# Moving one weight check and the first part of a tile across the block boundary

## The chip, the cores and the metric

The kernel runs on one core of one Trainium2 chip. The metric is the device time of the whole launch in microseconds (us); lower is better. A matmul engine (TensorE, PE in the rows), a vector engine (VectorE, DVE), a scalar engine (ScalarE, ACT), a general engine (GpSimd, POOL) and SyncE (SP, which here only issues DMAs) run their own instruction streams in order and meet through semaphores.

## The reference

The reference is a residual feed-forward layer whose input is a gated bidirectional recurrence along the sequence, for 4 batches of 1024 positions and 1024 channels:

```python
x = x + _L0_ffn_ref(_L0_cond_ref(x, fside, fside, w, u, cond), W1, W2)
# _L0_cond_ref: k = v = fside, r = x
ek = exp(min(k, 30)); ekv = ek * v
a, b = a * decay + ekv_t, b * decay + ek_t     # forward and backward over the 1024 positions
num = nf + nb - ekv + euk * v;  den = df + db - ek + euk
out = sigmoid(r) * (num / max(den, 1e-8)) * (0.8 + 0.2 * tf)
# _L0_ffn_ref: W1 (4096 x 1024), W2 (1024 x 4096), entries t * 2^-e, t in {-1, 0, 1}, e in 0..4
h = einsum('bsd,fd->bsf', x, W1)
a = gelu(clip(round(h / 0.1), ...) * 0.1)
return einsum('bsf,df->bsd', a, W2)
```

## The kernel before

**Blocks and tiles.** The 4 batches are cut into two halves of 512 positions each, which gives 8 blocks (n = 0 to 7). A block has 8 channel tiles of 128 channels x 512 positions. While block n goes through the feed-forward part, the recurrence of block n+1 is computed tile by tile on VectorE and ScalarE, so that TensorE finds its operands ready at the next block. Tiles are numbered through, g = 8 * block + t. In the even blocks a tile is "late" and needs the sums over the first half of the sequence as well, which costs two more activations on ScalarE (`exps`) and two more VectorE instructions (`weigh`).

**What a tile needs.** On ScalarE `tile_group(g)` issues the exponentials of tile g (`exps`), the logarithm and exponential that invert the denominator of tile g-1 (`reciprocal`, left out where g is the first tile of its block) and the exponential of the gate (`gate_exp`). On VectorE a tile is four parts: `part(0, g)` weighs the values, `part(1, g)` is the forward scan, `part(2, g)` the backward scan, `part(3, g)` the sums that free the tile's buffers. `mix(t, p, ...)` inside a block calls `part(p, g0 + t)`, where g0 = 8 * (n + 1) is the first tile of the next block; it does nothing in the last block.

**Feed-forward.** Each matmul is done in fp16 pieces (high and low), and most of the products are arranged as Winograd-like products of seven, with sums of operands made on VectorE. In a block from n = 1 on, TensorE starts with `products_15(n, 0)` (32 matmuls of 256 columns, line 754), whose first product is copied by ScalarE from one PSUM bank to another (`seed`, line 1098), and then does `products_26(n, 0)` (32 more), which accumulates on top of that copy and so waits for it: `pe.wait_ge(s_seed, q + 1)`. Then come `products_15(n, 1)`, `products_73(n, 0)`, `products_26(n, 1)`, `product_4(n, 0)` and so on. `product_4` waits for VectorE's `quantise22` (line 1622). At the end of a block the outputs 0 to 7 are made (line 897) and VectorE adds each to the residual and stages it (`residual_sum`, line 1698).

**Operands of the next block.** `operands_hi(n + 1, q)` on ScalarE (lines 1083 to 1086) and `convert(n + 1, q)` on VectorE (lines 1550 to 1565) make the matmul operands of quarter q of the next block, q = 0 to 3.

**The checks.** The kernel is exact only if the weights are multiples of 1/64 that fit in int8. So 64 slices of W1 and W2 (512 KB each) are checked on the way, 8 to a block, numbered `at` = 0 to 63. A check is a load into one buffer, `chk_full` (SyncE, `load_check`, line 502), a cast to int8 on ScalarE (`check_i8`, line 1183) and a comparison on VectorE that overwrites the buffer (`check`, line 1717). There is one buffer for it, so the load of check `at` waits until the comparison of `at - 1` is done:

```python
def load_check(at):
    if at > 0:
        sp.wait_ge(s_chk, at)
```

**Order.** All orders are written out by hand, in one stream for each engine. SyncE issues every load of the kernel in one order: the ring of eight weight slots (`ring_load`), the tiles, the residuals, the checks and the stores. Near the boundary its stream is, at the end of block n: store and residual loads, `load_check(at + 6)`, two ring loads; and at the start of block n+1: a ring load, `load_tile(g0 + 1)`, a ring load, then `load_check(at - 1)` with the new block's numbers. With `at` = 8 * n, the check called `at + 6` at the end of block n is the one called `at - 2` in block n+1.

Of the kernel before, what the change touches and what calls it, by code (L numbers as in the profile page):

```python
# [38 lines left out]
def adaln_ffn_kernel(nc, x, fside, cond, w, u, w1, w2, out):  # L39
    B, HALVES, CT, _, T = x.shape  # L40
# [5 lines left out]
    BLOCKS = B * HALVES  # L46
# [14 lines left out]
    with ExitStack() as ctx:  # L61
# [215 lines left out]
        def hid(n, s):  # L277

            return CHAIN * (n - 1) + (s if s <= SPLIT else s + 2)
# [724 lines left out]
        def _(act_e):  # L1004
# [52 lines left out]
            def tile_group(g):  # L1057

                exps(g, g - 1 if g % CT else g)
                if g % CT:  # L1060
                    reciprocal(g - 1, s_gate, g)
                gate_exp(g)
# [10 lines left out]
            def operands_hi(n, q):  # L1073
                g, at = CT * n + 2 * q, KH * (n - 1) + q
                slot = m_slot(g)
                act_e.wait_ge(s_out, g + 2)
                if n == 1:
                    act_e.wait_ge(s_h0, FT)
                    for k in range(2):
                        act_e.wait_ge(s_wstore[k], 16 * STEPS)  # L1080
                else:
                    act_e.wait_ge(s_p4, CHAIN * (n - 1))
                sc.activation(mo[:, B11, q, 0, :], m_quads[:, slot, 0, :], ACT.Copy).then_inc(s_mohi, 1)
                sc.activation(mo[:, B21:B22 + 1, q, 0, :], m_quads[:, slot, 2:4, :], ACT.Copy).then_inc(s_mohi, 1)
                act_e.wait_ge(s_t, 3 * at + 3)
                sc.activation(mo[:, T1:T4 + 1, q, 0, :], tt, ACT.Copy).then_inc(s_mohi, 1)
# [90 lines left out]
            def check_i8(at):  # L1177
                n = at // DT
                act_e.wait_ge(s_chkload, 16 * (at + 1))
                act_e.wait_ge(s_gelu, half_of(n, SPLIT - 1 if n > 0 and at % DT < 2 else LAST, 1) + 1)  # L1180
                if at > 0:
                    act_e.wait_ge(s_chk, at)
                sc.activation(chk_i8, chk_full[:, :], ACT.Copy, scale=W_SCALE).then_inc(s_chki8, 1)  # L1183
# [27 lines left out]
            def chained_block(n, nxt, g0, at):  # L1211
                seed(hid(n, 0))
                spill_p5(hid(n, 0))
                check_i8(at - 2)
                quantise11(n, 0)
                seed(hid(n, 1))
                spill_p5(hid(n, 1))
                check_i8(at - 1)
                quantise12(n, 0)
                if nxt:  # L1220
                    tile_group(g0 + 1)
                gelu(n, 0, 0)
                quantise11(n, 1)
                quads_hi_11(n, 0)
                for s in range(2, SPLIT + 1):
                    quantise21(n, s - 2)
                    gelu(n, s - 2, 1)
                    seed(hid(n, s))
                    quads_hi_2(n, s - 2)
                    spill_p5(hid(n, s))  # L1230
                    quads_hi_t(n, s - 2)
                    quantise12(n, s - 1)
                    gelu(n, s - 1, 0)
                    quantise11(n, s)
                    quads_hi_11(n, s - 1)

                quantise21(n, SPLIT - 1)
                gelu(n, SPLIT - 1, 1)
                quads_hi_2(n, SPLIT - 1)
                quads_hi_t(n, SPLIT - 1)  # L1240
                seed(part_y(n, 0))
                quantise12(n, SPLIT)
                gelu(n, SPLIT, 0)
                act_hi(n, SPLIT, 0)
                spill_p5(part_y(n, 0))
                if nxt:
                    tile_group_between(g0 + 2)
                quantise21(n, SPLIT)
                gelu(n, SPLIT, 1)
                act_hi(n, SPLIT, 1)  # L1250
                seed(part_y(n, 1))
                check_i8(at)
                spill_p5(part_y(n, 1))
                if nxt:
                    tile_group_between(g0 + 3)
                check_i8(at + 1)
                seed(hid(n, SPLIT + 1))
                spill_p5(hid(n, SPLIT + 1))
                if nxt:
                    tile_group(g0 + 4)  # L1260
                quantise11(n, SPLIT + 1)

                seed(hid(n, SPLIT + 2))
                spill_p5(hid(n, SPLIT + 2))
                if nxt:
                    tile_group(g0 + 5)
                quantise12(n, SPLIT + 1)
                gelu(n, SPLIT + 1, 0)
                quantise11(n, SPLIT + 2)
                act_hi(n, SPLIT + 1, 0)  # L1270
                quantise21(n, SPLIT + 1)
                gelu(n, SPLIT + 1, 1)
                seed(hid(n, LAST))
                act_hi(n, SPLIT + 1, 1)
                spill_p5(hid(n, LAST))
                quantise12(n, SPLIT + 2)
                gelu(n, SPLIT + 2, 0)
                quantise11(n, LAST)
                act_hi(n, SPLIT + 2, 0)

                quantise21(n, SPLIT + 2)
                gelu(n, SPLIT + 2, 1)
                act_hi(n, SPLIT + 2, 1)
                if nxt:
                    tile_group_between(g0 + 6)
                quantise12(n, LAST)
                gelu(n, LAST, 0)
                act_hi(n, LAST, 0)
                quantise21(n, LAST)
                gelu(n, LAST, 1)  # L1290
                act_hi(n, LAST, 1)
                if nxt:
                    operands_hi(n + 1, 0)
                check_i8(at + 2)
                if nxt:
                    tile_group_between(g0 + 7)
                    operands_hi(n + 1, 1)
                check_i8(at + 3)
                check_i8(at + 4)
                if nxt:  # L1300
                    reciprocal(g0 + 7, s_gate, g0 + 8)
                    operands_hi(n + 1, 2)
                    if n + 2 < BLOCKS:
                        tile_group(g0 + CT)
                    operands_hi(n + 1, 3)
                check_i8(at + 5)
                if not nxt:
                    check_i8(at + 6)
                    check_i8(at + 7)

            hidden_block0(CT)
# [11 lines left out]
            reciprocal(CT + 7, s_gate, CT + 8)  # L1323
            check_i8(5)
            operands_hi(1, 3)
            tile_group(2 * CT)
            for n in range(1, BLOCKS):
                chained_block(n, n + 1 < BLOCKS, CT * (n + 1), DT * n)
# [40 lines left out]
        def _(dve):  # L1369
# [149 lines left out]
            def part(p, g):  # L1519

                last = g - 1 if g % CT else None
                if p == 0:
                    weigh(g)
                if p == 1:
                    forward(g, last)
                if p == 2:
                    backward(g, last)
                if p == 3:
                    sums(g)
# [224 lines left out]
            def output_block0(g0):  # L1754
                weight_sums2(0)
                convert(1, 0)
                check(0)
                residual_sum(0, 0)
                part(3, g0 + 4)
                residual_sum(0, 1)  # L1760
                part(0, g0 + 5)
                check(1)
                convert(1, 1)
                weight_sums2(1)
                part(1, g0 + 5)
                residual_sum(0, 2)
                check(2)
                part(2, g0 + 5)
                part(3, g0 + 5)
                weight_sums2(2)  # L1770
                residual_sum(0, 3)
                part(0, g0 + 6)
                check(3)
                part(1, g0 + 6)
                part(2, g0 + 6)
                residual_sum(0, 4)
                part(3, g0 + 6)
                weight_sums2(3)
                part(0, g0 + 7)
                check(4)  # L1780
                part(1, g0 + 7)
                residual_sum(0, 5)
                part(2, g0 + 7)
                part(3, g0 + 7)
                convert(1, 2)
                divide(g0 + 7)
                check(5)
                convert(1, 3)
                residual_sum(0, 6)
                part(0, g0 + CT)  # L1790
                residual_sum(0, 7)

            def chained_block(n, nxt, g0, at):
                def mix(t, *parts):
                    if nxt:
                        for p in parts:
                            part(p, g0 + t)

                seed_u4(hid(n, 0))
                check(at - 2)  # L1800
                mix(0, 1, 2)
                quantise22(n, 0)
                check(at - 1)
# [93 lines left out]
                    convert(n + 1, 3)  # L1897
                    check(at + 5)
                residual_sum(n, 6)
                if n + 2 < BLOCKS:  # L1900
                    part(0, g0 + CT)
                if nxt:
                    residual_sum(n, 7)

            hidden_block0(CT)
# [142 lines left out]
```

## Time and profile before

| | |
|---|---|
| time, median of 3 runs | 1751.11 us (1750.88 to 1751.9) |
| time of the profiled execution | 1751.11 us |
| its span, first to last instruction | 1748.8 us |
| TensorE busy | 1655.3 us (95% of the span) |
| VectorE busy | 1292.6 us (74%) |
| ScalarE busy | 933.8 us (53%) |
| mean granted TensorE clock | 0.986 |
| DMA queue of SyncE | 351.86 MB, 60.6% of 16 engines |

The profiled execution took 1751.11 us, of which 1748.8 us lie between its first and last instruction. A busy share is the share of the span in which at least one instruction of the engine ran. The time in brackets at the end of a row of the timeline is the idle time of that engine just ahead of the row, with the instruction that ended it.

### The profile page before, as it was taken

What the parts mean: (1) busy time and instruction counts of PE and PEld (TensorE: products, weight loads), DVE (VectorE), ACT (ScalarE), POOL (GpSimd) and SP (SyncE); (2) the same over time, 40 slices, a digit from 0 to 9 for tenths busy, and PEclk for the clock granted to TensorE, in tenths of its full rate; (3) what the DMA queues carried; (4) which work ended last, traced back from release to release, by engine and by line L of the source; (5) the groups of instructions that cost most, each with busy time, mean ns of one, the idle gap of its engine ahead of it and who ended that gap; (6) DMA issues with size and microseconds to landing.
All of it is one profiled execution on the core that took longest, in us unless ns stands there. A gap on an engine that the chain in (4) does not pass through costs nothing. (4 is left out here: it accounts for less than half of the span.)

```text
span 1748.8 us, 30785 instructions
## 1 busy us (share of the span) xinstructions
PE 1655.3 (95%) x12258; PEld 1201.0 (69%) x12258; DVE 1292.6 (74%) x1787; ACT 933.8 (53%) x1450; POOL 24.6 (1%) x44
## 2 busy tenths in 40 slices
PE   1579999899999999999999999999999999999998
PEld 0134444688748886688847887488866888478874
DVE  8977877589697867888787876978778776755222
ACT  3457522574746646385655646467464755455141
POOL 0000020000000000000000000000000000000000
PEclk9789999999999999999999999999999999999999
DMA  9858785768556684757747585676847677465744
GB/s 246 196 159 241 282 298 190 247 195 288 175 211 213 217 268 136 262 183 269 241 142 252 183 271 167 217 233 222 286 137 256 185 251 232 158 206 181 234 135 158
DMA packets 153461, 376.97 MB, mean 216 GB/s; under 512 B 15328, under 2 KB 44256, under 8 KB 152800
## 3 DMA queue, kind: packets, MB, share of 16 engines
q1 hardware_dynamic: 150624, 351.86, 60.6%
q0 software_dynamic: 2688, 23.07, 5.8%
q8 instruction: 99, 1.62, 0.4%
q14 instruction: 50, 0.41, 0.1%
HBM read 347.61 MB, written 67.11 MB: 237 GB/s over the span
## 5 line engine op out<-in xcount | busy, mean ns | idle before, releaser
L754 PE MATMUL ps<-mo,w_ring 128*128 128x256 f16 x6272 | 698.7, 273 | 13.1 <-ACT ps L1098 5.7
L754 PEld LDWEIGHTS ps<-mo,w_ring 128*128 128x128 f16 x6272 | 613.6, 98 | 93.7 <-issue 16.0
L897 PE MATMUL ps<-act,w_ring 128*128 128x512 f16 x1760 | 383.3, 380 | 0.0
L817 PE MATMUL ps<-act,w_ring 128*128 128x256 f16 x3136 | 348.1, 273 | 0.0
L817 PEld LDWEIGHTS ps<-act,w_ring 128*128 128x128 f16 x3136 | 306.0, 98 | 36.3
L897 PEld LDWEIGHTS ps<-act,w_ring 128*128 128x128 f16 x1760 | 172.0, 98 | 203.4
L1654 DVE SCALAR_TENSOR_TENSOR act<-a,act 128x1024 f16<-128x1024 f32 x72 | 88.0, 1222 | 95.9 <-ACT act L1158 95.9
L1183 ACT ACTIVATE q<-tt 128x1024 int8<-128x1024 f32 x64 | 67.2, 1050 | 160.7 <-DMA tt<-in_w_dram 160.7
L1148 ACT ACTIVATE a<-q 128x1024 f32<-128x1024 int16 x128 | 135.3, 1057 | 15.7 <-DVE act L1654 10.7
L1098 ACT ACTIVATE ps<-ps 128x512 f32<-128x512 f32 x70 | 40.7, 581 | 153.3 <-PE ps L754 89.5
L1717 DVE SCALAR_TENSOR_TENSOR tt<-q,tt 128x1024 f32<-128x1024 int8 x64 | 78.1, 1221 | 49.0 <-ACT q L1183 49.0
L883 PE MATMUL ps<-act,w_ring 128*128 128x512 f16 x512 | 110.8, 380 | 3.0 <-DVE xy L1698 3.0
L1610 DVE SCALAR_TENSOR_TENSOR ps<-sp,ps 128x512 f32<-128x512 f32 x70 | 48.5, 693 | 85.7 <-issue 43.3
L731 PE MATMUL ps<-mo,w_ring 128*128 128x512 f16 x128 | 42.7, 511 | 71.5 <-DVE mo L1539 71.5
L883 PEld LDWEIGHTS ps<-act,w_ring 128*128 128x128 f16 x512 | 50.0, 98 | 63.7 <-issue 3.4
L1512 DVE SCALAR_TENSOR_TENSOR ND<-EE,bonus,ND 128x1024 f32<-128x1024 f32 x64 | 81.9, 1280 | 1.6
L744 PE MATMUL ps<-mo,w_ring 128*128 128x512 f16 x384 | 83.0, 380 | 0.0
L731 PEld LDWEIGHTS ps<-mo,w_ring 128*128 128x128 f16 x128 | 15.5, 125 | 98.3 <-issue 51.3
L1492 DVE TENSOR_TENSOR_SCAN ND<-decay,back,ND 128x512 f32<-128x512 f32 x64 | 81.9, 1280 | 0.6
L1496 DVE TENSOR_TENSOR_SCAN ND<-decay,back,ND 128x512 f32<-128x512 f32 x64 | 81.7, 1276 | 0.0
L1665 DVE TENSOR_TENSOR tt<-a 128x1024 f32<-128x1024 f32 x28 | 34.3, 1225 | 58.8 <-ACT a L1148 58.8
L1158 ACT ACTIVATE act<-a 128x1024 f16<-128x1024 f32 x72 | 75.8, 1053 | 1.4
(121 smaller groups left out, 1653.4 us busy)
## 6 DMA issues: line engine op xcount, KB each, us to landing
w_ring<-w1s SPq DMA_DIRECT2D x168, 512.0 KB, 4.8
w_ring<-w_half SPq DMA_DIRECT2D x130, 512.0 KB, 5.1
tt<-in_w_dram SPq DMA_DIRECT2D x64, 512.0 KB, 5.3
w_ring<-w2s SPq DMA_DIRECT2D x56, 512.0 KB, 4.9
V<-in_fside_dram SPq DMA_DIRECT2D x64, 256.0 KB, 5.8
R<-in_x_dram SPq DMA_DIRECT2D x64, 256.0 KB, 5.9
w_half<-in_w_dram POOLq DMA_DIRECT2D x16, 1024.0 KB, 8.2
xy<-in_x_dram SPq DMA_DIRECT2D x64, 256.0 KB, 4.9
```

The lines of the kernel that those rows point to most:

```text
L744: mm = pe.matmul(bank[4 * (s % 2) + j][:, :], w1_ring[:, k, f, c, :], mix0[:, c, p, :], start=(c == 0 and p == 0), stop=(c == CT - 1 and p ...
L754: mm = pe.matmul(dst[:, f, :], wp_ring[:, k, r, f, q, :], mo[:, op, q, p, :], start=(fresh and f == 0 and q == 0 and p == 0), stop=(q == K ...
L817: mm = pe.matmul(dst[:, i, :], wy_ring[:, k, i, 2 * s + j, :], ao[:, s, op, j, p, :], start=(fresh and i == 0 and s == 0 and j == 0 and p ...
L883: mm = pe.matmul(y_ps[y][:, :], w2_ring[:, k, f, :], act[:, FPS * s + j, p, :], start=(h == 0 and f == 0 and p == 0), stop=(h == 1 and f = ...
L897: mm = pe.matmul(bank[d][:, :], w2_ring[:, k, FPS * (s - SPLIT) + j, :], act[:, act_at(n, s) + j, p, :], start=(s == SPLIT and j == 0 and ...
L1148: sc.activation(a32[:, 2 * h:2 * h + 2, :], q16[:, s % 2, 2 * h:2 * h + 2, :], ACT.Gelu_apprx_tanh, scale=QSTEP).then_inc(s_gelu, 1)
L1158: sc.activation(act[:, f:f + 2, 0, :], a32[:, 2 * h:2 * h + 2, :], ACT.Copy, scale=ACT_SCALE).then_inc(s_ahi, 1)
L1492: v.tensor_tensor_scan(DEN[:, k, :][:, ::-1], dec(b, c), DEN[:, k, :][:, ::-1], back[:, k, 1:2], ALU.mult, ALU.add).then_inc(s_dbwd, 1)
L1496: v.tensor_tensor_scan(NUM[:, k, :][:, ::-1], dec(b, c), NUM[:, k, :][:, ::-1], back[:, k, 0:1], ALU.mult, ALU.add).then_inc(s_nbwd, 1)
L1512: v.scalar_tensor_tensor(out=ND[:, k, :, :], in0=EE[:, k, :, :], scalar=bonus[:, b, c:c + 1], in1=ND[:, k, :, :], op0=ALU.mult, op1=ALU.ad ...
L1654: v.scalar_tensor_tensor(out=act[:, f:f + 2, 1, :], in0=a32[:, 2 * h:2 * h + 2, :], scalar=ACT_SCALE, in1=act[:, f:f + 2, 0, :], op0=ALU.m ...
L1717: v.scalar_tensor_tensor(out=chk_full[:, :], in0=chk_i8, scalar=1.0 / W_SCALE, in1=chk_full[:, :], op0=ALU.mult, op1=ALU.not_equal, accum_ ...
```

## The change

Three things move, and nothing is added or removed. No load is moved on SyncE.

1. Check 6 of a block (`at + 6`, on ScalarE and on VectorE) is done at the end of its own block and no longer at the start of the next one. On ScalarE it used to stand behind the next block's first `seed` and `spill_p5`; it now stands ahead of them. On VectorE it used to stand behind `seed_u4(hid(n, 0))`; it now stands ahead of `residual_sum(n, 7)` of the block before. This holds for the seven boundaries into blocks 1 to 7.
2. On ScalarE `tile_group(g0 + CT)`, the first tile of the block after the next, moves from between `operands_hi(n + 1, 2)` and `operands_hi(n + 1, 3)` to behind check `at + 6`. In block 0 it stood behind `operands_hi(1, 3)` already, and check 6 now comes ahead of it.
3. On VectorE `part(0, g0 + CT)` moves from ahead of `residual_sum(n, 7)` to the first place of the next block, where it is written `mix(0, 0)`.

```diff
@@ ScalarE, chained_block, start
                 seed(hid(n, 0))
                 spill_p5(hid(n, 0))
-                check_i8(at - 2)
                 quantise11(n, 0)
@@ ScalarE, chained_block, end
                 if nxt:
                     reciprocal(g0 + 7, s_gate, g0 + 8)
                     operands_hi(n + 1, 2)
-                    if n + 2 < BLOCKS:
-                        tile_group(g0 + CT)
                     operands_hi(n + 1, 3)
                 check_i8(at + 5)
+                check_i8(at + 6)
+                if n + 2 < BLOCKS:
+                    tile_group(g0 + CT)
                 if not nxt:
-                    check_i8(at + 6)
                     check_i8(at + 7)
@@ ScalarE, after block 0
             check_i8(5)
             operands_hi(1, 3)
+            check_i8(6)
             tile_group(2 * CT)
@@ VectorE, output_block0
                 residual_sum(0, 6)
-                part(0, g0 + CT)
+                check(6)
                 residual_sum(0, 7)
@@ VectorE, chained_block, start
+                mix(0, 0)
                 seed_u4(hid(n, 0))
-                check(at - 2)
                 mix(0, 1, 2)
@@ VectorE, chained_block, end
                 residual_sum(n, 6)
-                if n + 2 < BLOCKS:
-                    part(0, g0 + CT)
                 if nxt:
+                    check(at + 6)
                     residual_sum(n, 7)
```

## Rows read from the trace of the kernel before

**Rows 1.** Waits of TensorE from 330 us on: total us, times, longest.

```profile
PE ps L754 <- DVE q L1622: 4.4, 6, 0.9
PE ps L754 <- ACT ps L1098: 3.0, 3, 1.4
```

**Rows 2.** Timeline of TensorE, starts of blocks 2 to 7 (start us, us, what).

```profile
522.26 26.36 PE L754 MATMUL ps<-mo,w_ring 128*128 128x256 f16 x240
550.03 3.65 PE L754 MATMUL ps<-mo,w_ring 128*128 128x256 f16 x32 [1.40 <-ACT ps L1098]
...
726.87 26.36 PE L754 MATMUL ps<-mo,w_ring 128*128 128x256 f16 x240
...
930.27 26.62 PE L754 MATMUL ps<-mo,w_ring 128*128 128x256 f16 x240
...
1135.11 29.86 PE L754 MATMUL ps<-mo,w_ring 128*128 128x256 f16 x272
...
1337.71 22.54 PE L754 MATMUL ps<-mo,w_ring 128*128 128x256 f16 x205
...
1540.59 19.60 PE L754 MATMUL ps<-mo,w_ring 128*128 128x256 f16 x178
```

**Rows 3.** Timeline of ScalarE at the boundary into block 2.

```profile
518.71 0.61 ACT L1031 ACTIVATE EE<-V 128x512 f32<-128x512 f32 x1
...
520.55 0.40 ACT L1083 ACTIVATE mo<-m_st 128x256 f16<-128x256 f32 x1
...
524.21 0.58 ACT L1098 ACTIVATE ps<-ps 128x512 f32<-128x512 f32 x1
...
529.67 1.06 ACT L1183 ACTIVATE q<-tt 128x1024 int8<-128x1024 f32 x1 [3.11 <-DMA tt<-in_w_dram]
530.63 0.58 ACT L1119 ACTIVATE q<-ps 128x512 int16<-128x512 f32 x1
```

**Rows 4.** Timeline of SyncE: issue of the loads of checks 6 and 7.

```profile
525.70 0.33 SPq L502 DMA_DIRECT2D tt<-in_w_dram  x1
...
532.02 0.33 SPq L502 DMA_DIRECT2D tt<-in_w_dram  x1
```

**Rows 5.** Timeline of VectorE: checks 5 and 7 at the same boundary.

```profile
524.45 1.22 DVE L1717 SCALAR_TENSOR_TENSOR tt<-q,tt 128x1024 f32<-128x1024 int8 x1
...
539.36 1.22 DVE L1717 SCALAR_TENSOR_TENSOR tt<-q,tt 128x1024 f32<-128x1024 int8 x1 [1.78 <-ACT q L1183]
```

**Rows 6.** Timeline of ScalarE: a late tile's group, and check 6 into blocks 3 to 7.

```profile
720.35 0.61 ACT L1027 ACTIVATE EKP<-VP 128x512 f32<-128x512 f32 x1
...
723.32 0.40 ACT L1083 ACTIVATE mo<-m_st 128x256 f16<-128x256 f32 x1
...
731.75 1.06 ACT L1183 ACTIVATE q<-tt 128x1024 int8<-128x1024 f32 x1 [0.59 <-DMA tt<-in_w_dram]
...
938.04 1.06 ACT L1183 ACTIVATE q<-tt 128x1024 int8<-128x1024 f32 x1 [3.22 <-DMA tt<-in_w_dram]
...
1139.77 1.06 ACT L1183 ACTIVATE q<-tt 128x1024 int8<-128x1024 f32 x1 [0.37 <-DMA tt<-in_w_dram]
...
1344.73 1.06 ACT L1183 ACTIVATE q<-tt 128x1024 int8<-128x1024 f32 x1 [2.73 <-DMA tt<-in_w_dram]
...
1545.24 1.06 ACT L1183 ACTIVATE q<-tt 128x1024 int8<-128x1024 f32 x1 [0.36 <-DMA tt<-in_w_dram]
```

**Rows 7.** Timeline of TensorE: three stretches after an idle wait, one without.

```profile
57.07 5.95 PE L731 MATMUL ps<-mo,w_ring 128*128 128x512 f16 x16 [6.91 <-DVE mo L1539]
69.00 5.11 PE L731 MATMUL ps<-mo,w_ring 128*128 128x512 f16 x16 [5.98 <-DVE mo L1539]
...
313.67 5.32 PE L754 MATMUL ps<-mo,w_ring 128*128 128x256 f16 x32 [2.92 <-DVE xy L1698]
...
461.77 3.62 PE L897 MATMUL ps<-act,w_ring 128*128 128x512 f16 x16
```

**Rows 8.** One window: busy us (count) of PE, PEld, DVE, ACT, POOL; granted clock; DMA; GB/s.

```profile
316.00:317.00 1.00, 1.00 (x6) 0.68 (x5) 0.00 (x0) 0.00 (x0) 0.00 (x0) 0.50 1.07 412
```

## The prediction

> **What bounds the kernel now.** I read the share of busy time first (TensorE 95%), then the waits of TensorE, then its timeline at each start of a block, and then the timelines of ScalarE, VectorE and SyncE around those points. After 330 us, in seven chained blocks, TensorE waits 3.0 us in all for ScalarE's `seed` and 4.4 us for VectorE's `quantise22` [rows 1]. That is 7.4 us, and nothing else: the rest is matmuls back to back, 240 of 256 columns in 26.36 us, 0.110 us each [rows 2]. So TensorE sets the time in every block. The most that any reordering of the other engines can give there is 7.4 us (0.4%), while each new stall of TensorE counts in full.
>
> Where are the 7.4 us? In block 2 the first is 1.40 us ahead of `products_26(2, 2)`, some 27 us into the block [rows 2], on the third `seed`. It comes from the check numbered `at - 1` (check 7): its load is issued at 532.02 [rows 4], 9.8 us after the start of the block at 522.26 [rows 2], because it had to wait until the comparison of check 6 was done. VectorE waited 1.78 us for the cast and compared at 539.36 [rows 5]; its sums for the tile, ScalarE's reciprocal, the gelu and the third seed follow one another behind it. So check 6 at the start of the block does cost something, a little at a time, and the change aims at that.
>
> **What is taken away.** With check 6 done in the block before, the load of check 7 waits only for the ring load ahead of it on SyncE, which goes with the end of `products_26(n, 0)`: two groups of 32 matmuls, 2 x 3.5 = 7.0 us of TensorE's own time after the start of the block, where it was 9.8. So check 7 and all behind it come about 2.7 us earlier relative to TensorE. The waits of block 2 are the largest, 1.4 + 0.9 = 2.3 us [rows 1, 2]; I take all 7.4 us of waits as gone. Bounds: 0 if another link of that chain is late, 7.4 if none is.
>
> **What is added, on ScalarE's queue.** This is the term that matters. `seed(hid(n, 0))` used to stand ahead of check 6. Now `check_i8(at + 6)` and, into blocks 2 to 6, `tile_group` stand ahead of it, in an engine that works in order, and that check waits for a load. TensorE wants the seed after its first 32 matmuls, 3.5 us after the start of the block. Queued behind it are `products_26(n, 0)` and everything after it; TensorE has no other work to take.
>
> When does the load land? It needs the comparison of check 5, one buffer for both. That comparison starts at 524.45 and lasts 1.22 us [rows 5]; the load goes out at 525.70 [rows 4], already 3.4 us into the new block; ScalarE starts the cast at 529.67, having waited 3.11 us for the DMA [rows 3]. That is 4.0 us from issue to cast. None of it moves up: SyncE's order is untouched, and VectorE reaches check 5 when it has done `convert(n + 1, 3)`, which on an early tile waits for VectorE's own sums and not for `tile_group`. So the cast of check 6 starts at the same time after the change as before, and I only have to hang the rest behind it:
>
> - the cast holds ScalarE for 530.63 - 529.67 = 0.96 us [rows 3];
> - `tile_group` holds it 520.55 - 518.71 = 1.84 us for an early tile [rows 3], 723.32 - 720.35 = 2.97 us for a late one [rows 6];
> - the seed lasts 0.58 us [rows 3], 0.60 with the hand-over.
>
> The stall is (start of the cast + 0.96 + tile + 0.60) - (start of the block + 3.5), the casts and blocks from [rows 2, 3, 6]:
>
> - into block 2, early: 529.67 + 3.40 = 533.07, wanted at 525.76: 7.3 us
> - into block 3, late: 731.75 + 4.53 = 736.28, wanted at 730.37: 5.9 us
> - into block 4, early: 938.04 + 3.40 = 941.44, wanted at 933.77: 7.7 us
> - into block 5, late: 1139.77 + 4.53 = 1144.30, wanted at 1138.61: 5.7 us
> - into block 6, early: 1344.73 + 3.40 = 1348.13, wanted at 1341.21: 6.9 us
> - into block 7, no tile: 1545.24 + 1.56 = 1546.80, wanted at 1544.09: 2.7 us
>
> Sum 36.2 us. On a late tile `operands_hi(n + 1, 3)` comes 3 us earlier on ScalarE and may pull check 5 up by a few tenths; that is at most 1 us in the sum and I leave it. Into block 1 nothing changes: `tile_group` stood ahead of the seed already, held by a tile load, and check 6 fits in while it waits.
>
> **What is added, on VectorE.** Check 6 (1.22 us [rows 5]) now stands ahead of `residual_sum(n, 7)`, and that now waits for the cast: into block 2 until 529.67 + 1.06, so the sum ends near 532.7. TensorE needs it for `products_15(n + 1, 1)`, which now starts at 533.07 + 3.5. Covered by the stall itself, cost 0; without the stall it would be wanted at 529.3 and would cost 3.4 us. `part(0)` goes ahead of `seed_u4(hid(n, 0))`, which waits for the end of `products_26(n, 0)` anyway: cost 0.
>
> **What is added, by the clock.** TensorE's granted clock falls after waits of this size. After an idle wait of 2.92 us, 32 matmuls took 5.32 us [rows 7] where they take 3.65 us [rows 2]: 1.67 us lost, with a granted clock of 0.50 in that stretch [rows 8], that is 1.2 GHz in place of 2.4. After waits of 5.98 and 6.91 us, 16 matmuls of 512 columns took 5.11 and 5.95 us against 3.62 [rows 7]: 1.5 and 2.3 us lost. I take 1.9 us for each of the five long stalls and 1.67 for the one of 2.7 us: 9.5 + 1.7 = 11.2 us. Bounds: 0, if the slow stretch fell inside the stall, and 6 x 2.3 = 14. The Trainium skill (TensorE: Matmul & The Clock Gate, "HAM oscillation — how this bites in real kernels") works out a case in which TensorE cools down in every DMA wait and pays 26.7 us over 32 waits, 0.83 us each. By it six waits would cost 5.0 us and the sum would be 6.2 us smaller; the rows here show twice that.
>
> **Sum.** 36.2 - 7.4 + 11.2 = 40.0 us. The profiled execution took 1751.11 us, which is also the median; 1751.11 + 40.0 = 1791.1 us, slower by 2.3%.
>
> **The rivals.**
>
> *The clock costs little (chance 0.07).* The slow stretch lies inside a stall of 6 to 8 us and TensorE restarts at 2.4 GHz. For it: a stall longer than those of [rows 7] leaves more room for that. Against it: in [rows 7] the longest wait had the largest loss. Time: 1791.1 - 11.2 = 1779.9 us. By the figure of the skill's page above it would be 1784.9 us.
>
> *The old waits stay, or the load lands later (0.10).* If ScalarE, delayed at the seed, is the late link for the rest of the chain, the 7.4 us are not given back: 1798.5 us. If the load took as long as that of check 7 does (532.02 to the cast, which ends just ahead of 539.36 and so starts at about 538.3, 6.3 us) instead of 4.0, six stalls grow by 2.3 us: 1804.9 us. Against the second: in the old kernel this very load was measured at the same place, in front of the same neighbours in the queue.
>
> *The other side: the stall does not appear and only the gain is left (0.04).* The seed is in time if the cast starts by 3.5 - 0.60 - 1.84 - 0.96 = 0.1 us into the block on an early tile. For that the load must be issued some 4 us before the block starts; it goes out 3.4 us after (525.70 against 522.26). It would need VectorE to reach check 5 over 7 us earlier, which could only be if the end of the block were held by `tile_group`; [rows 3] show no wait for it: the cast of check 5 is done before the seed at 524.21, two us after the block's start, and VectorE compares at once. Time: 1751.1 - 7.4 = 1743.7 us.
>
> *No change (0.02).* A stall of about 1.2 us a boundary would cancel the 7.4 us: the load would have to be on its way 6 us sooner. 1751 us.
>
> **How the numbers follow.** The forecast has the rest, 0.77, with its own range 1784 to 1798 us from the clock's 1.5 to 2.3 us a stall and some tenths in each stall. The range for 8 in 10 takes in the clock's lower bound and the return of the old waits: 1779 to 1799 us. About 0.2% (3.5 us) is what a measurement of this kernel can tell from no change. Slower by more than that: 0.77 + 0.07 + 0.10 = 0.94. Faster 0.04. Same 0.02.
>
> **What would show each step.** In the profile after: TensorE's waits for ScalarE line 1098 grow from 3 to some 37 us over six places, each after exactly 32 matmuls of a block, five of 5.5 to 8 us and the last near 2.7; early tiles stall longer than late ones by about 1.5 us. ScalarE's wait for the check's load stands directly ahead of the tile's exponentials, and the seed behind them. The wait for `quantise22` and the one some 27 us into a block are gone. The granted clock is 0.50 in parts of the first microseconds after each stall. The prediction is wrong if check 5's comparison comes at another place in the block, if the load takes other than 4.0 us, or if the gaps later in the block do not close.

## The result

The changed kernel takes 1791.87 us (median of 4 runs, 1790.1 to 1793.43) against 1751.29 us (median of 4 runs) for the kernel before: a ratio of 1.0231, 95% interval 1.0213 to 1.0249. The profiled execution took 1789.21 us; its span is 1786.9 us where it was 1748.8 us, so 38.1 us are to be found in the trace. It was the fastest execution of the changed kernel: the medians differ by 40.6 us.

The waits of TensorE from 330 us on, in the changed kernel (who waited for whom: us in total, times, longest):

```profile
PE ps L754 <- ACT ps L1098: 35.2, 6, 7.3
PE ps L754 <- DVE mo L1560: 0.5, 1, 0.5
```

These two lines stand where [rows 1] stood. The wait for `quantise22` (4.4 us) is gone, the wait for the seed has gone from 3.0 to 35.2 us. The timeline of TensorE shows where (block 2, then the restart after the stall into blocks 3 to 7):

```profile
521.94 3.66 PE L754 MATMUL ps<-mo,w_ring 128*128 128x256 f16 x32
532.80 54.33 PE L754 MATMUL ps<-mo,w_ring 128*128 128x256 f16 x480 [7.21 <-ACT ps L1098]
...
742.45 55.29 PE L754 MATMUL ps<-mo,w_ring 128*128 128x256 f16 x480 [5.75 <-ACT ps L1098]
...
955.58 54.56 PE L754 MATMUL ps<-mo,w_ring 128*128 128x256 f16 x480 [7.27 <-ACT ps L1098]
...
1165.06 53.93 PE L754 MATMUL ps<-mo,w_ring 128*128 128x256 f16 x480 [5.35 <-ACT ps L1098]
...
1375.54 54.49 PE L754 MATMUL ps<-mo,w_ring 128*128 128x256 f16 x480 [6.97 <-ACT ps L1098]
...
1582.28 52.56 PE L754 MATMUL ps<-mo,w_ring 128*128 128x256 f16 x480 [2.67 <-ACT ps L1098]
```

Each block starts with 32 matmuls, stalls, and then runs 480 without a gap, through both places where it used to wait. Read the stalls down: 7.21, 5.75, 7.27, 5.35, 6.97 and 2.67 us, in all 35.2. Read the durations of the 480: the last block needs 52.56 us, and the others 1.77, 2.73, 2.00, 1.37 and 1.93 us more, in all 9.8. That is the clock. Four windows around and behind the end of the first stall, which ends at 532.80 (window: its length, then busy us and count of PE, PEld, DVE, ACT and POOL, then the granted clock, the DMA share and GB/s):

```profile
532.00:534.00 2.00, 1.20 (x6) 0.89 (x7) 0.80 (x2) 1.17 (x4) 0.00 (x0) 0.50 0.89 348
534.00:536.00 2.00, 2.00 (x12) 1.41 (x10) 0.00 (x0) 0.00 (x0) 0.00 (x0) 0.50 0.00 0
536.00:538.00 2.00, 2.00 (x18) 1.72 (x17) 0.00 (x0) 0.60 (x1) 0.00 (x0) 0.89 0.00 0
538.00:540.00 2.00, 2.00 (x21) 1.79 (x19) 1.69 (x2) 0.00 (x0) 0.00 (x0) 1.00 0.29 67
```

The granted clock is 0.50 (1.2 GHz) in the first two windows and in part of the third; the second window touches 12 matmuls, the fourth, at the full clock, 21. Now the queue of ScalarE at the same boundary, to be laid beside [rows 3]:

```profile
522.82 1.04 ACT L1183 ACTIVATE q<-tt 128x1024 int8<-128x1024 f32 x1
529.28 1.06 ACT L1183 ACTIVATE q<-tt 128x1024 int8<-128x1024 f32 x1 [5.42 <-DMA tt<-in_w_dram]
530.24 0.61 ACT L1031 ACTIVATE EE<-V 128x512 f32<-128x512 f32 x1
...
532.08 0.57 ACT L1098 ACTIVATE ps<-ps 128x512 f32<-128x512 f32 x1
```

The cast of check 6 waits 5.42 us for its load with the seed queued behind it; then come the tile's exponentials, 1.84 us, and only then the seed. On SyncE the load goes out at 525.35, 3.4 us into the block, and lands 3.9 us later; check 7's load follows at 538.62, right behind the ring load:

```profile
525.35 0.33 SPq L502 DMA_DIRECT2D tt<-in_w_dram  x1
...
538.25 0.33 SPq L437 DMA_DIRECT2D w_ring<-w1s  x1
538.62 0.44 SPq L502 DMA_DIRECT2D tt<-in_w_dram  x1
```

The balance is 35.2 (stalls) + 0.5 (the wait in block 4 for `operands_lo`, a part of VectorE's `convert`) - 7.4 (old waits) + 9.8 (clock) = 38.1 us, which is the growth of the span. What the sum leaves out is some tenths: block 2 starts 0.3 us sooner (521.94 against 522.26), for instance. The wait of 0.5 us need not come from the change, since runs 8 and 9, with ScalarE's cast of check 6 and the later tiles as in the kernel before, have one of 0.3 us at the same place.

### The profile page after: what moved, and what is told of

Its sections match the earlier page's. It is cut to its first block and busy times, and to the rows that moved or that the text cites. A ratio compares the mean times of both kernels' runs of the same rounds, so it can differ in the third digit from the quotient of the medians.

```text
span 1786.9 us, 30785 instructions
## 1 busy us (share of the span) xinstructions
PE 1667.1 (93%) x12258; PEld 1207.4 (68%) x12258; DVE 1292.8 (72%) x1787; ACT 934.3 (52%) x1450; POOL 24.7 (1%) x44
## 5 line engine op out<-in xcount | busy, mean ns | idle before, releaser
L754 PE MATMUL ps<-mo,w_ring 128*128 128x256 f16 x6272 | 706.4, 275 | 41.1 <-ACT ps L1098 39.6
L1098 ACT ACTIVATE ps<-ps 128x512 f32<-128x512 f32 x70 | 40.6, 581 | 156.6 <-PE ps L754 100.4
```

Source lines behind the costliest of these rows:

```text
L754: mm = pe.matmul(dst[:, f, :], wp_ring[:, k, r, f, q, :], mo[:, op, q, p, :], start=(fresh and f == 0 and q == 0 and p == 0), stop=(q == K ...
```

## The experiments

All ratios are to the kernel before, timed beside it on the same chip; their 95% intervals stand in brackets.

**1. ScalarE back, VectorE changed.** The changed kernel with the whole ScalarE program of the kernel before. Its core:

```diff
                 seed(hid(n, 0))
                 spill_p5(hid(n, 0))
+                check_i8(at - 2)
                 quantise11(n, 0)
...
                     operands_hi(n + 1, 2)
+                    if n + 2 < BLOCKS:
+                        tile_group(g0 + CT)
                     operands_hi(n + 1, 3)
                 check_i8(at + 5)
-                check_i8(at + 6)
-                if n + 2 < BLOCKS:
-                    tile_group(g0 + CT)
```

> Only VectorE has the order of the changed kernel; ScalarE has the order of the kernel before, with the seed ahead of the cast of check 6. Theory (the queue on ScalarE is the cost): the six stalls of 2.7 to 7.3 us after the first 32 matmuls of a block are gone. What is left is VectorE's own term: residual_sum(n, 7) waits for the cast and is late for products_15(n + 1, 1), by about 3.4 us into the early blocks 2, 4, 6 and by 0.5 us into 3, 5, 7, some 11 us, with some 5 us for the clock after the three longer ones, less up to 7.4 us of old waits: 1751 + 9 = 1760 us, between 1755 and 1767. Rival (VectorE's order or the check's new place as such is the cost): near 1790 us.

Measured: 1761.61 us, ratio 1.0060 (1.0042 to 1.0077). TensorE's waits from 330 us on:

```profile
PE ps L754 <- DVE xy L1698: 11.4, 6, 3.4
PE ps L754 <- DVE q L1622: 1.8, 2, 0.9
```

Two places of its timeline, in blocks 2 and 4:

```profile
533.35 49.07 PE L754 MATMUL ps<-mo,w_ring 128*128 128x256 f16 x448 [3.21 <-DVE xy L1698]
...
943.72 50.73 PE L754 MATMUL ps<-mo,w_ring 128*128 128x256 f16 x448 [3.42 <-DVE xy L1698]
```

No wait for the seed is left. In its place stands the term that the prediction had costed at nothing behind the stall and at 3.4 us without it: `residual_sum(n, 7)`, queued on VectorE behind the comparison of check 6. It is 11.4 us in six waits. So ScalarE's order back takes away three quarters of the loss, and a second stall was waiting beneath the first. Of the 5 us set down for the clock, 3.3 came: 448 matmuls took 49.07 us behind the wait of 3.21 us, 50.73 behind the one of 3.42 and 50.72 behind one of 2.99 us in block 6.

**2. VectorE back, ScalarE changed.** The other half alone (VectorE: `check(at - 2)` behind `seed_u4`, `part(0, ...)` ahead of `residual_sum(n, 7)`, as before).

```diff
-                mix(0, 0)
                 seed_u4(hid(n, 0))
+                check(at - 2)
...
                 residual_sum(n, 6)
+                if n + 2 < BLOCKS:
+                    part(0, g0 + CT)
                 if nxt:
-                    check(at + 6)
                     residual_sum(n, 7)
```

> Only ScalarE has the order of the changed kernel; VectorE has the order of the kernel before. Theory: all six stalls stay as they are, since the cast and the tile's exponentials stand ahead of the seed; the comparison of check 6 comes after seed_u4, about 8 us later, and the load of check 7 about 1.5 us later, which the delayed TensorE hides: 1791 us, between 1788 and 1797. Rival (VectorE's order is the cost): near 1751 us.

Measured: 1792.76 us, ratio 1.0235 (1.0218 to 1.0252), the same as the changed kernel. TensorE's waits from 330 us on:

```profile
PE ps L754 <- ACT ps L1098: 34.9, 6, 7.5
PE ps L754 <- DVE q L1622: 1.4, 3, 0.5
```

The stalls are all there, as foretold. But 6.0 us of the old 7.4 us of waits are gone too, although VectorE compares check 6 where it used to. Into block 2 the load of check 7 leaves at 543.47, 18.7 us after the block's first matmul at 524.76. Without the stall (7.21 us) and the slow clock (2.35 us) that is 9.2 us of TensorE's own time, where it was 9.8 us in the kernel before and is 7.7 us in the changed one. So a load of check 7 that leaves almost as late as before still makes no wait in block 2. The likely reason is the stall, which holds TensorE back while the other engines go on; no run separates this from the cast of check 6 being out of ScalarE's way by then. The 1.4 us that stay are in blocks 1, 3 and 5. The two halves don't add up (0.6% and 2.35% against 2.31%), since the one stall covers the other.

**3. The tile out of the way.** The changed kernel, with only the cast ahead of the seed:

```diff
                     operands_hi(n + 1, 2)
+                    if n + 2 < BLOCKS:
+                        tile_group(g0 + CT)
                     operands_hi(n + 1, 3)
                 check_i8(at + 5)
                 check_i8(at + 6)
-                if n + 2 < BLOCKS:
-                    tile_group(g0 + CT)
```

> The changed kernel, with the tile's exponentials back between operands_hi(n + 1, 2) and operands_hi(n + 1, 3) on ScalarE; only the cast stays ahead of the seed. Theory: each stall shrinks by the tile's time, 3 x 1.84 + 2 x 2.97 = 11.5 us, and the clock gives back little: 1780 us, between 1776 and 1783. The stalls are then about 5.4, 2.9, 5.8, 2.7, 5.1 and 2.7 us. Rival (the tile's exponentials would be done in the DMA wait for nothing, so their place doesn't matter): 1792 us.

Measured: 1775.14 us, ratio 1.0139 (1.0123 to 1.0156), a little below the range that I gave. TensorE's timeline, blocks 2, 3 and 5:

```profile
533.25 54.07 PE L754 MATMUL ps<-mo,w_ring 128*128 128x256 f16 x480 [5.45 <-ACT ps L1098]
...
739.63 52.56 PE L754 MATMUL ps<-mo,w_ring 128*128 128x256 f16 x480 [2.73 <-ACT ps L1098]
...
1155.21 52.56 PE L754 MATMUL ps<-mo,w_ring 128*128 128x256 f16 x480 [2.86 <-ACT ps L1098]
```

The stalls are as foretold (24.3 us in all, 35.2 - 24.3 = 10.9 of the 11.5 expected). What I had put too low is in the durations: after stalls of 2.7 and 2.9 us the 480 matmuls take 52.56 us, with no loss by the clock, where after 5.75 and 5.35 us they had lost 2.73 and 1.37 us. So the shorter stalls gave back clock too: in all six blocks the 480 matmuls lost 5.6 us, where they had lost 9.8.

**4. Matmuls into the stall.** The changed kernel, with one product of the first 32 matmuls done four times in blocks 2 to 6, so that TensorE has 5.3 us of needless work in each stall:

```diff
+                for _ in range(3 if s == 0 and 2 <= n < BLOCKS - 1 else 0):
+                    product(halves[at + 2], k, 1, T1, True, (lambda q: ready + 3 * q + 3))
                 product(halves[at + 2], k, 1, T1, True,
```

> The changed kernel, with product T1 of products_15(n, 0) done four times instead of once in blocks 2 to 6 (240 more matmuls of 256 columns, 5.3 us in each of these blocks at 2.4 GHz; the result is the same). TensorE so works through most of each stall. Theory (some 10 us of the loss are matmuls at 1.2 GHz after the stalls): the idle time shrinks to 0.1 to 2.0 us a block, the granted clock stays at 1, and the kernel gets faster by about 9.8 us in spite of the added work: 1782 us, between 1779 and 1785. Rival (the clock is no part of the loss): 1792 us or more.

Measured: 1782.43 us, ratio 1.0180 (1.0163 to 1.0197). 240 matmuls more, and faster than the changed kernel (1.0231) by half a per cent, some 9 us. Two rows of TensorE, blocks 2 and 6:

```profile
536.14 52.56 PE L754 MATMUL ps<-mo,w_ring 128*128 128x256 f16 x480 [2.06 <-ACT ps L1100]
...
1369.48 54.23 PE L754 MATMUL ps<-mo,w_ring 128*128 128x256 f16 x480 [1.97 <-ACT ps L1100]
```

The waits for the seed are down from 35.2 to 8.9 us, which is just the 26.3 us of added matmuls (240 at 0.110 us), so the time gained is not idle time. In blocks 2 to 6 the idle time in front of the 480 matmuls is 0 to 2.1 us, and behind it they take 52.56 us in block 2. The expectation of a full clock throughout missed in block 6, where they still lost 1.67 us. The clock's share of the loss is shown: most of the 9.8 us went when the stalls were filled.

**5. A small check 6 in the changed kernel.** Load, cast and comparison of check 6 only take 64 of the 1024 columns; the others of these seven slices are left out.

The load (the cast and the comparison take the same `cols`):

```diff
+                cols = 64 if at % DT == 6 and at // DT < BLOCKS - 1 else 2 * T
-                sp.dma_start(chk_full[:, :], full[at // 4 % STEPS].rearrange("p (i m) -> i p m", i=4)[at % 4]).then_inc(
+                sp.dma_start(chk_full[:, 0:cols], full[at // 4 % STEPS].rearrange("p (i m) -> i p m", i=4)[at % 4][:, 0:cols]).then_inc(
...
```

> The changed kernel, with check 6 of blocks 0 to 6 cut to 64 of its 1024 columns (load, cast and comparison; 960 columns of these seven slices are left unchecked). Theory (the stall is load + cast + tile in line): the cast shrinks by about 0.8 us and the load from 4.0 us to some 2 to 2.5 us, so that each of six stalls shrinks by 2.3 to 2.8 us, 14 to 17 us in all, and the last, of 2.7 us, goes with its clock loss: 1775 us, between 1770 and 1780. Rival (the load is not what the cast waits for in the line, or lands with its neighbours in the queue whatever its size): 1787 us, the cast's 0.8 us alone.

Measured: 1769.37 us, ratio 1.0097 (1.0082 to 1.0113), just below my range. SyncE and then ScalarE at the boundary into block 2:

```profile
525.46 0.33 SPq L503 DMA_DIRECT2D tt<-in_w_dram  x1
```

```profile
527.26 0.26 ACT L1185 ACTIVATE q<-tt 128x64 int8<-128x64 f32 x1 [3.29 <-DMA tt<-in_w_dram]
527.42 0.61 ACT L1032 ACTIVATE EE<-V 128x512 f32<-128x512 f32 x1
...
529.26 0.57 ACT L1099 ACTIVATE ps<-ps 128x512 f32<-128x512 f32 x1
```

The load of 32 KB is there after 1.8 us instead of 3.9, less than the 2 to 2.5 us that I had assumed, and the cast holds ScalarE for 0.16 us instead of 0.96. Each link in front of the seed counts in full: into block 2 the stall is 4.28 us in place of 7.21, shorter by the 2.1 us of the load and the 0.8 us of the cast. In all the waits for the seed fell from 35.2 to 18.7 us. What is left is the tile, the short load itself and that it goes out only at 525.46, behind the comparison of check 5.

**6. A small check 6 in the kernel before.** The same 64 columns there, again with the rest of the seven slices unchecked.

> The kernel before, with check 6 of blocks 0 to 6 cut to 64 of its 1024 columns in the same way. Theory (the 7.4 us of waits come from check 6 through check 7's load): the comparison of check 6 ends up to 1.2 us earlier and the load of check 7 leaves at the ring load, 2 us sooner: 4 to 7 us faster, 1744 to 1747 us. Rival (other work makes these waits): 1751 us.

Measured: 1743.32 us, ratio 0.9954 (0.9938 to 0.9969), some 8 us faster and just beyond the 4 to 7 us expected. TensorE's waits from 330 us on:

```profile
PE ps L755 <- DVE q L1624: 0.9, 1, 0.9
PE ps L755 <- ACT ps L1099: 0.3, 1, 0.3
```

Of 7.4 us, 1.2 are left. So the old waits did come from check 6. That this went by way of check 7's load fits runs 2 and 7, but this run alone doesn't separate it from the cast and the comparison, which are shorter here too. The rest of the 8 us is of two kinds. Block 2 starts 1.1 us sooner (521.15 against 522.26), 0.5 us of it a wait in block 1 that is already counted. At the start of block 1 this profile has one wait of 4.38 us and the kernel before has two, of 2.92 us [rows 7] and 2.72 us (under run 9); that place varies from profile to profile in all of these kernels, and I don't count it. From block 2 on, each wait that goes gives back a little more than its length, since 32 matmuls between two waits take 3.65 us and in a stream 26.36 / 240 x 32 = 3.51 us: for six waits about 1 us.

**7. Check 7 later, instead.** From the kernel before; a way to the same 7.4 us that puts nothing in front of the seed:

```diff
                 spill_p5(hid(n, 1))
-                check_i8(at - 1)
                 quantise12(n, 0)
                 if nxt:
                     tile_group(g0 + 1)
+                check_i8(at - 1)
...
                 quantise22(n, 0)
-                check(at - 1)
                 mix(0, 3)
                 seed_u4(hid(n, 1))
+                check(at - 1)
```

> The kernel before, with check 6 where it was and check 7 moved instead, inside the block's start: on ScalarE from ahead of quantise12(n, 0) to behind tile_group(g0 + 1), on VectorE from ahead of mix(0, 3) to behind seed_u4(hid(n, 1)), where VectorE sat idle. Theory (the old waits come from the chain load of check 7, cast, comparison, sums, reciprocal, gelu, seed): the tile's sums no longer wait for the load and come about 2 us sooner, no seed waits, 5 to 7 us gained: 1745 us, between 1743.5 and 1747. Rival (the chain is as long by ScalarE's own work): 1751 us.

Measured: 1747.50 us, ratio 0.9976 (0.9967 to 0.9985): some 4 us faster, a little less than the 5 to 7 us expected. From 330 us on TensorE's waits for the seed are gone, and 1.9 us are left:

```profile
PE ps L754 <- DVE q L1622: 1.9, 5, 0.5
```

**8. Only VectorE's check 6 earlier**, ahead of `seed_u4(hid(n, 0))`, from the kernel before.

> The kernel before, with only VectorE's comparison of check 6 moved ahead of seed_u4(hid(n, 0)), where VectorE waits for TensorE anyway. Theory: into the late blocks 3 and 5 the load of check 7 leaves up to 1.6 us sooner and their waits of 1.1 and 0.5 us go, into the early ones nothing changes: 1749.6 us, between 1748.5 and 1751. Rival (seed_u4 is late for products_73): slower by 1 us or more.

Measured: 1749.79 us against 1752.04, ratio 0.9990 (0.9981 to 0.9999). The size fits; it is at the edge of what can be told from nothing. The places don't fit: in its profile the seed's wait in block 2, which was to stay, is 0.21 us in place of 1.40, and block 3 still waits 0.60 us of its 1.1. So the theory of this move is not shown.

**9. The seed first in block 1 too.** The kernel before has one boundary at which ScalarE already had work that waits for a load ahead of the seed: `tile_group(2 * CT)` into block 1.

```diff
             operands_hi(1, 3)
-            tile_group(2 * CT)
...
                 spill_p5(hid(n, 0))
+                if n == 1:
+                    tile_group(2 * CT)
                 check_i8(at - 2)
```

> The kernel before, with one move on ScalarE at the boundary into block 1: tile_group(2 * CT), which waits there for a tile's load, goes from ahead of the seed to behind the seed and spill_p5 of block 1. It is the reverse of what the change does at the other boundaries. Theory (work that waits for a load, ahead of the seed, is what stalls TensorE): the wait for the seed of 2.7 us in block 1 and its stretch at 1.2 GHz (1.4 us) go, the tile's comparison work behind has room: 3 to 5 us faster, about 1747 us against 1751. Rival (what is delayed by it, the tile and the residual sum behind it, holds TensorE as long): no change.

Measured: 1747.03 us, ratio 0.9972 (0.9961 to 0.9982), 5 us faster. TensorE in block 1, first in the kernel before (behind the 32 matmuls of [rows 7]):

```profile
321.71 27.78 PE L754 MATMUL ps<-mo,w_ring 128*128 128x256 f16 x240 [2.72 <-ACT ps L1098]
```

and with the seed first:

```profile
316.14 26.36 PE L754 MATMUL ps<-mo,w_ring 128*128 128x256 f16 x240 [2.15 <-DVE xy L1699]
343.85 3.65 PE L754 MATMUL ps<-mo,w_ring 128*128 128x256 f16 x32 [1.34 <-ACT ps L1098]
348.41 26.36 PE L754 MATMUL ps<-mo,w_ring 128*128 128x256 f16 x240 [0.91 <-DVE q L1623]
```

The wait for the first seed and the slow clock behind it are gone: 240 matmuls run in 26.36 us from the start. Part of it comes back as the two waits of 1.34 and 0.91 us; I take it that the tile is now late for the chain further on, which no run separates. From block 1's first matmul of line 754 to its first of line 817 it is 58.5 us (316.14 to 374.61) where it was 62.5 us (313.67 to 376.18), 4.0 us less. Of these, 1.67 us are the slow 32 matmuls of [rows 7], behind a wait for `residual_sum` that the move doesn't touch. The profiled execution was the slowest of the eight and started block 1 2.5 us later, so its span is only 1.4 us shorter.

**10. Both moves** (the seventh and the ninth run together).

> The kernel before, with check 7 later (as in the seventh run) and the seed of block 1 ahead of the tile. If the two gains are independent: 4.5 us from the first (its measured ratio 0.9976) plus 3 to 5 us, a ratio of 0.995, 1742 to 1745 us. Rival (the second only moves the wait elsewhere): the same as the seventh run, ratio 0.9976.

Measured: 1742.45 us, ratio 0.9949 (0.9935 to 0.9962). The gains add up, and this version beats both kernels, the changed one by 2.8%.

**11. All three moves** (with the eighth).

> As the run of both moves, and VectorE's comparison of check 6 ahead of seed_u4(hid(n, 0)). Check 7 is no longer in the chain that this would shorten, so no further gain: within 0.1% of the run of both moves. If it is faster by more, the load of check 7 is still in the chain.

Measured: 1744.10 us, ratio 0.9955 (0.9942 to 0.9969), no different from the two. That fits the theory that with check 7 out of the chain there is nothing left for it to shorten.

## Why the prediction was right, and where its sizes were off

- **The bound.** TensorE sets the time in every block and only 7.4 us were to be had: right from 330 us on, where it was counted, and all of it was given back, as the 480 matmuls without a gap show. The start of block 1 lies outside that count, with waits of 2.92 and 2.72 us and 3.1 us of slow clock, and run 9 gains 5 us there.
- **The way it was given back.** The prediction put it down to check 7's load, 2.7 us earlier in TensorE's own time; it came 2.1 us earlier (7.7 us into block 2 in place of 9.8). The sixth run shows that check 6 was the source of the old waits in the kernel before. But run 2, with the load only 0.6 us earlier into block 2, has 6.0 of the 7.4 us gone as well. So most of it goes without the earlier load, probably since the stall holds TensorE back: the number was right, and the reason given for it is not the one that carried it there.
- **The stalls.** Forecast 7.3, 5.9, 7.7, 5.7, 6.9, 2.7 us, measured 7.21, 5.75, 7.27, 5.35, 6.97, 2.67. The step that carried this was that the cast would start at the same time as before the change. At the boundary into block 2 it did, 7.3 us after the block's first matmul (529.28 - 521.94) where it had been 7.4 us. Runs 3 and 5 show two of the links, the tile and the load with its cast, one by one. Into block 1 check 6 is not what holds the seed, as foretold: its cast starts at 311.72, and the tile's exponentials wait for their own load until 318.35 (317.87 before). The wait for the seed there is 4.37 us in place of 2.72, but the one just ahead of it 0.89 in place of 2.92.
- **VectorE.** `residual_sum(n, 7)` was said to be covered by the stall, and to cost 3.4 us in an early block without it; run 1 gives 3.21 us in block 2 and 3.42 us in block 4.
- **The clock.** Forecast 11.2 us, measured 9.8. Five stalls lost 1.96 us each on average, against 1.9 taken; the sixth, of 2.67 us, lost nothing, where I had put 1.67 us by the 2.92 us wait of [rows 7]. That is the one term whose size was clearly off. The Trainium skill's case (0.83 us a wait, page "TensorE: Matmul & The Clock Gate", section "HAM oscillation — how this bites in real kernels") would have given 5.0 us; this kernel's trace shows twice that.
- **Left out.** The wait of 0.54 us for `operands_lo` among the first matmuls of block 4; too small to matter.
- **The sum.** Forecast 40.0 us, found in the trace 38.1, in the medians 40.6. That the median (1791.87 us) lies within 1 us of 1791.1 is partly luck: the single terms were off by 1.0 us (stalls) and 1.4 us (clock), and executions of the changed kernel differ by 4 us.

Of the rivals, the forecast had the cheap clock at 1779.9 us. Run 4 removes most of that term and comes to 1782.43 us, which bears out its size. The load did not land later in the block than before (the cast starts after 7.3 us in place of 7.4 in block 2), so 1804.9 us did not come about. The other side (1743.7 us) would have needed the seed in time. Nor did the old waits stay (1798.5 us).

## What to carry to other kernels

An in-order engine with slack on the average has none in front of an instruction that the bounding engine waits for. Before moving work across such an instruction, look at when the moved work can run, not how long it takes: here, in run 3, 0.96 us of cast cost 2.7 to 5.6 us a block, since its data was still on the way. To gain from a late link, take out of the chain the item that others wait for (check 7) rather than bring the one ahead of it forward; and look for other places with the same pattern, such as block 1 here.

## What the runs showed of the hardware that was not expected

In these runs the price of a stall in TensorE's clock is not a smooth function of its length. Stalls of 2.67 us (changed kernel), 2.73 and 2.86 us (run 3) and 3.21 us (run 1) were followed by matmuls at full speed (52.56 us for 480, 49.07 us for 448), while one of 2.92 us in the kernel before lost 1.67 us [rows 7], and one of only 1.97 us, in run 4, also lost 1.67 us. A stall of 3.51 us in run 5 lost 2.6 us (55.17 us for 480), more than one of 7.27 us in the changed kernel, 2.00. Stalls of 5.4 to 7.3 us in the changed kernel lost 1.4 to 2.7 us each, without order by length.

The windows show where the difference lies. First the changed kernel into block 2 (TensorE restarts at 532.80), then run 4 in block 6 (restart at 1369.48), then run 5 in block 3 (restart at 737.29):

```profile
529.00:530.00 1.00, 0.00 (x0) 0.00 (x0) 0.00 (x0) 0.72 (x1) 0.00 (x0) 0.81 0.97 373
536.00:537.00 1.00, 1.00 (x9) 0.82 (x8) 0.00 (x0) 0.59 (x1) 0.00 (x0) 0.78 0.00 0
...
1369.00:1370.00 1.00, 0.52 (x5) 0.50 (x6) 0.48 (x1) 0.85 (x2) 0.00 (x0) 1.00 0.83 283
1370.00:1371.00 1.00, 1.00 (x9) 0.76 (x8) 0.00 (x0) 0.00 (x0) 0.00 (x0) 0.69 1.02 401
1373.00:1374.00 1.00, 1.00 (x8) 0.71 (x7) 0.00 (x0) 0.00 (x0) 0.00 (x0) 0.60 0.00 0
...
735.00:736.00 1.00, 0.00 (x0) 0.00 (x0) 0.46 (x1) 1.00 (x4) 0.00 (x0) 0.93 0.91 324
742.00:743.00 1.00, 1.00 (x8) 0.78 (x7) 0.00 (x0) 0.00 (x0) 0.00 (x0) 0.66 0.00 0
```

The granted clock is 0.50 between the first and the last window of each group. In the changed kernel it falls some 3 us ahead of the restart, so nearly half of the slow stretch lies in the stall and costs nothing. In run 4 it is still at 1.00 through the stall of 1.97 us and falls only behind the restart, so that all of the slow stretch is paid for. In run 5 it falls little more than 1 us ahead of the restart and stays low over 5 us behind it. So a stall is paid for by the part of the slow stretch that lies behind it; the runs don't show what decides when the clock falls and for how long.
